# ScalarE's PSUM ring as four single banks, with exponentials, projections and the first MLP product in smaller units

## The chip, the cores and the metric

One core of a Trainium2 chip. The metric is device time in microseconds for one execution of the whole program; the median of several runs counts, and one more execution is profiled.

## The reference, cut to what matters

A PixArt-like stack over 16 items of 256 tokens with 128 channels, in float32. Layer 0, then an expert layer, then layers 2 and 3. Attention has 16 heads of 8 channels. Cross-attention goes to a context of 1601 tokens, self-attention to the item's own 256:

```python
def _attend(q, k, v):
    attn = jnp.einsum('bhnd,bhsd->bhns', q, k) * SCALE
    attn = jax.nn.softmax(attn, axis=-1)
    o = jnp.einsum('bhns,bhsd->bhnd', attn, v)
```

Around it stand layer norms with modulation by the item's condition, a projection with gate and residual, and in layers 0 and 3 an MLP of 512 hidden channels with a tanh GELU. Layer 0 has self- and cross-attention, layer 2 cross-attention, layer 3 both.

## The kernel before, in words

The function attention_phase runs twice: "pa" for layer 0, and "pb" for layers 2 and 3; the expert layer stands between them. Each phase carries two streams: "c", the cross-attention items (16 in pa, 32 in pb, 1601 keys in 13 tiles of 128, the last with 65), and "z", the self-attention items (16 in each, 256 keys). Each item goes through tokens: ln, xt (transpose), q, ctx (transposes of the context), k, v, M (maxima), Rn and Rt (the maxima as rows), S and T (scores), V (product with the values), oev and o (output moved and divided), ot, proj, and with an MLP ln2, x2t, h, tanh, gm, fc2. The function body_plan places the tokens of several items in one repeated body by the fractions of the PLACES tables, stage_list unrolls it, and merge_maxima moves the M tokens by a small model of the engines (class Clocks, with the work tables PE_WORK, ACT_WORK and DVE_WORK). Every engine walks the resulting list PROG in its order and waits on semaphores; so on each engine a waiting instruction holds up all behind it.

PSUM has eight banks. The ring of ScalarE (ACT) is two units of two banks, aunit, with RING_A = 2: every token of ACT_RING takes one unit, whether it fills 1024 columns or 256. VectorE's ring is three single banks (dbank), and one bank (obank) gathers the outputs of V. TensorE waits until the unit two tokens back has been emptied (a_free), writes, and signals a_full; ScalarE empties it and signals a_free.

A score unit S is four bf16 matmuls of 256 columns, two key tiles by two halves of the rows ("par"), and par is the bank of the unit. Its exponential is one instruction of 1024 columns (line 778). T is the same for the last tile. V is four float32 matmuls, in the trace as eight records, of one key tile. M is two matmuls of 512 columns in two banks of VectorE's ring, for stream z four of 256. The products ctx, k and v go in groups of 8 and 5 tiles (s.groups), h is eight records into 1024 columns with four evictions; GpSimd (POOL) then makes the cubic in z, and ScalarE the tanh.

An item of stream c has 48 S and 4 T, an item of stream z 8 S; the phases have 960 and 1792 such units.

## Time and profile before

| | |
|---|---|
| median of 3 runs | 5283.68 us (5279.14 to 5287.49) |
| span of the profiled execution | 5282.2 us |
| phase pa, about | 0 to 1740 us of the span |
| expert layer, about | 1740 to 2360 us |
| phase pb, about | 2360 to 5282 us |

The profiled execution has no time of its own beside its span; the span is 1.5 us under the median of the runs. Busy time of an engine is the union of its instructions. PE is TensorE's matmul side and PEld its weight loads; ends of pipelined matmuls are modelled, so matmuls that drain count as busy. DVE is VectorE, ACT ScalarE, POOL GpSimd. A wait is put down to the instruction whose signal came last.

### The profile page before, as it was taken

The page shows a single profiled execution, that of the slowest core. Times are in us where ns is not written, and L with a number is a line of the kernel's source. Part 1 is how long each engine was busy: PE and PEld are TensorE (multiplying, and loading weights), DVE is VectorE, ACT ScalarE, POOL GpSimd, SP SyncE. Part 2 cuts the span into 40 slices and gives each one's busy share as a digit, 9 for nine tenths or more (in the row PEclk, how much of TensorE's full clock was granted, in tenths as well). Part 3 has the DMA queues.
Part 4 walks back from the last instruction along what each step waited for, and adds up shares of the span by engine and source line. Part 5 has one row for each costly group of instructions (what it writes and reads, how often), then busy time and mean ns, then how long its engine had stood idle before and what let it go on. Part 6 is the DMA issues. An engine that isn't in the chain of part 4 may idle for free.

```text
span 5282.2 us, 123295 instructions
## 1 busy us (share of the span) xinstructions
PE 4674.1 (88%) x47956; PEld 2177.8 (41%) x47956; DVE 4160.5 (79%) x8997; ACT 3597.9 (68%) x4899; POOL 1667.0 (32%) x2339
## 2 busy tenths in 40 slices
PE   3799999999999588866999999999999999999997
PEld 1244444444443377752333333333333443333333
DVE  4598888888888244445999999999888888888884
ACT  1377777777777344432777777777787777777776
POOL 3443443443341100014233333242323233223321
PEclk9699999999999799986999999999999999999998
DMA  2221211211210111111121212121121211111110
GB/s 51 61 65 49 67 54 49 68 52 50 65 38 29 46 34 34 29 30 58 45 61 53 69 52 69 54 63 55 55 70 52 64 44 58 50 54 57 43 48 8
DMA packets 362976, 271.12 MB, mean 51 GB/s; under 512 B 47911, under 2 KB 325002, under 8 KB 362396
## 3 DMA queue, kind: packets, MB, share of 16 engines
q1 hardware_dynamic: 362396, 263.23, 17.3%
q8 instruction: 383, 6.28, 0.5%
q14 instruction: 197, 1.61, 0.1%
HBM read 86.96 MB, written 12.78 MB: 19 GB/s over the span
## 4 chain that ended last, share of the span: by engine, by line
PE 38%; DVE 7%; ACT 5%; issue 4%; POOL 0%; SPq 0%; DMA 0%; ACTq 0%; POOLq 0%; DVEq 0%
PE pb_obank L1027 14%; PE pb_dbank L1040 9%; PE pb_aunit L1003 6%; DVE pb_c_maxs L699 5%; ACT pb_probs L778 4%; PE pb_aunit L1081 2%; PE pb_aunit L1074 1%; PE pb_aunit L1066 1%; PE pb_dbank L1088 1%; PE pb_aunit L1114 1%; PE pb_aunit L1108 1%; PE pb_aunit L1011 1%; PE pb_aunit L1098 1%; DVE pb_c_mbf L709 1%; PE pb_aunit L1048 0%
## 5 line engine op out<-in xcount | busy, mean ns | idle before, releaser
L699 DVE TENSOR_REDUCE pb_c_maxs<-pb_dbank 128x1 f32<-128x512 f32 (+1 forms) x3584 | 2045.5, 627 | 312.2 <-PE pb_dbank L1040 293.4
L778 ACT ACTIVATE pb_probs<-pb_aunit 128x1024 f32<-128x1024 f32 (+1 forms) x1792 | 1761.6, 1024 | 276.2 <-PE pb_aunit L1003 223.8
L699 DVE TENSOR_REDUCE pa_c_maxs<-pa_dbank 128x1 f32<-128x512 f32 (+1 forms) x1792 | 1028.3, 627 | 181.5 <-PE pa_dbank L1040 167.6
L778 ACT ACTIVATE pa_probs<-pa_aunit 128x1024 f32<-128x1024 f32 (+1 forms) x960 | 937.4, 1024 | 194.9 <-PE pa_aunit L1003 160.6
L1027 PE MATMUL pb_obank<-pb_probs,pb_c_vaug 128*9 128x256 f32 x13312 | 945.6, 381 | 2.8 <-ACT pb_probs L778 0.2
L1040 PE MATMUL pb_dbank<-pb_c_kst,pb_c_qst 62*128 62x512 bf16 (+1 forms) x4096 | 760.6, 341 | 104.6 <-DVE pb_c_maxs L699 87.5
L1003 PE MATMUL pb_aunit<-pb_c_qst,pb_c_kst 64*128 64x256 bf16 x6144 | 581.2, 272 | 64.2 <-ACT pb_probs L778 40.6
L1040 PEld LDWEIGHTS pb_dbank<-pb_c_kst,pb_c_qst 62*128 62x128 bf16 x4096 | 227.7, 93 | 649.0 <-DVE pb_c_maxs L699 466.3
L1027 PE MATMUL pa_obank<-pa_probs,pa_c_vaug 128*9 128x256 f32 x6656 | 467.0, 381 | 1.3 <-ACT pa_probs L778 0.8
L1040 PE MATMUL pa_dbank<-pa_c_kst,pa_c_qst 62*128 62x512 bf16 (+1 forms) x2048 | 405.1, 348 | 44.9 <-DVE pa_c_maxs L699 21.1
L1027 PEld LDWEIGHTS pb_obank<-pb_probs,pb_c_vaug 128*9 128x9 f32 x13312 | 243.1, 89 | 372.3 <-issue 207.0
L1003 PEld LDWEIGHTS pb_aunit<-pb_c_qst,pb_c_kst 64*128 64x128 bf16 x6144 | 239.1, 95 | 338.8 <-ACT pb_probs L778 135.3
L1003 PE MATMUL pa_aunit<-pa_c_qst,pa_c_kst 64*128 64x256 bf16 x3072 | 289.3, 273 | 28.2 <-ACT pa_probs L778 17.6
L1040 PEld LDWEIGHTS pa_dbank<-pa_c_kst,pa_c_qst 62*128 62x128 bf16 x2048 | 116.4, 94 | 333.1 <-DVE pa_c_maxs L699 209.1
L699 DVE TENSOR_REDUCE pa_z_maxs<-pa_dbank 128x2 f32<-128x512 f32 x256 | 164.0, 684 | 51.9 <-PE pa_dbank L1040 51.5
L1027 PEld LDWEIGHTS pa_obank<-pa_probs,pa_c_vaug 128*9 128x9 f32 x6656 | 124.9, 89 | 181.8 <-issue 99.8
L1003 PEld LDWEIGHTS pa_aunit<-pa_c_qst,pa_c_kst 64*128 64x128 bf16 x3072 | 119.6, 95 | 163.5 <-ACT pa_probs L778 68.1
L699 DVE TENSOR_REDUCE pb_z_maxs<-pb_dbank 128x2 f32<-128x512 f32 x256 | 164.8, 686 | 11.7 <-PE pb_dbank L1040 8.8
L932 POOL TENSOR_TENSOR pb_z_x1a<-pb_z_x1a,pb_l_self_bo_rows 128x256 f32<-128x256 f32 x16 | 11.7, 731 | 490.8 <-ACT pb_z_x1a L848 490.8
L920 POOL CAST pb_c_ksp<-pb_c_kf 128x1024 bf16<-128x1024 f32 x64 | 54.5, 852 | 309.8 <-ACT pb_c_kf L821 309.8
L1532 DVE SCALAR_TENSOR_TENSOR moe_hh<-moe_ht,moe_hz 128x512 f32<-128x512 f32 x48 | 33.2, 692 | 123.6 <-ACT moe_ht L1626 122.8
L1658 POOL TENSOR_SCALAR moe_g<-moe_g2t 128x256 f32<-128x256 f32 x16 | 6.5, 406 | 369.5 <-ACT moe_g2t L1630 369.5
(475 smaller groups left out, 6737.6 us busy)
## 6 DMA issues: line engine op xcount, KB each, us to landing
pb_c_kst<-pb_c_ksp SPq DMA_DIRECT2D x384, 200.1 KB
pa_c_kst<-pa_c_ksp SPq DMA_DIRECT2D x192, 200.1 KB
pb_c_cin<-in_ctx SPq DMA_DIRECT2D x32, 768.0 KB
pa_c_cin<-in_ctx SPq DMA_DIRECT2D x16, 768.0 KB
moe_cin<-in_ctx SPq DMA_DIRECT2D x16, 768.0 KB
pb_c_qst<-pb_c_qsp SPq DMA_DIRECT2D x384, 32.0 KB
pa_z_qst<-pa_z_qsp SPq DMA_DIRECT2D x192, 32.0 KB
pa_z_kst<-pa_z_ksp SPq DMA_DIRECT2D x192, 32.0 KB
```

The lines of the kernel that those rows point to most:

```text
L699: dve.tensor_reduce(dst, dbank[N % RING_D][:, 0:cnt * width].rearrange("p (s c) -> p s c", s=cnt), AX.X, ALU.max).then_inc(d_free, 1)
L709: dve.tensor_copy(s.mbf[half][:], s.negm[half][:]).then_inc(s.m_bf, 1)
L778: act.activation(probs[u % RING_P][0:rows].rearrange("p a i q -> p (a i q)"), src[0:rows, :], ACT.Exp, scale=HD ** -0.5).then_inc(a_free, 1)
L920: pool.tensor_copy(s.ksp[:, 0, part], s.kf[:, part]).then_inc(s.k_hi, 1)
L1003: ins = pe.matmul(dst[:, par * 512 + h * NQ:par * 512 + (h + 1) * NQ], s.kst[b2][lo:lo + ROWS, pair, t * P:(t + 1) * P], s.qst[b2][lo:lo + ...
L1011: ins = pe.matmul(dst[0:s.last, par * 512 + pp * NQ:par * 512 + (pp + 1) * NQ], s.kst[b2][lo:lo + ROWS, 2 * q + pp, (s.kt - 1) * P:s.keys] ...
L1027: ins = pe.matmul(obank[32 * h4:32 * h4 + HD + 1, half * NQ:(half + 1) * NQ], s.vaug[i % 2][:, t, 4 * q + h4, :], src, start=(t == 0), sto ...
L1040: ins = pe.matmul(dbank[nd[tok, s.key, i, par] % RING_D][:, col:col + width], s.qst[b2][lo:lo + MAX_ROW, p, qt * P:(qt + 1) * P], s.kst[b2 ...
L1066: ins = pe.transpose(dst[:, (t - t0) * P:(t - t0) * P + rows], s.cin[0:rows, t, :], ident[0:rows, 0:rows])
L1074: ins = pe.matmul(dst[:, at - t0 * P:at - t0 * P + width], w.wkp[:], src[:, at:at + width], start=True, stop=True)
L1081: ins = pe.matmul(dst[0:rows, (t - t0) * P:(t - t0 + 1) * P], (s.srct if s.has_ctx else s.xmt)[:, t * P:t * P + rows], w.wv[:], start=True ...
L1088: ins = pe.transpose(dbank[N % RING_D][:, g * P:(g + 1) * P], s.osb[:, g, qt * P:(qt + 1) * P], ident[:])
```

## The change

ACT's ring becomes four single banks, abank, with RING_A = 4. S and T (TWO_BANKS) take two consecutive banks of the ring; every other token takes one. TensorE waits for the first bank ahead of the unit's first matmul and for the second ahead of its second, and signals each bank after its last matmul. ScalarE makes the exponential of each bank by itself, 512 columns, and frees each bank by itself. The groups of ctx, k and v become 4, 4, 4 and 1 tiles (GROUP = 4), and h two tokens of 512 columns, with GpSimd's part halved along with it; tanh stays one instruction. The added tokens stand 0.02 of a body behind their neighbours in PLACES. The work tables follow, Clocks knows single banks, and merge_maxima may now pull V tokens whose exponentials are done ahead of an S or T that would wait more than STALL.

```diff
@@ -169,8 +169,9 @@
         link.join()
 
 
-RING_A = 2
+RING_A = 4
 RING_D = 3
+GROUP = 4
 RING_P = 6
 K_ROWS = 48
...
-        self.groups = [(0, min(8, self.kt))] + ([(8, self.kt - 8)] if self.kt > 8 else [])
+        self.groups = [(t, min(GROUP, self.kt - t)) for t in range(0, self.kt, GROUP)]
...
-          "ca": 0.1616, "xt": 0.1932, "ln2": 0.1973, "v1": 0.2369, "st1": 0.2929, "q": 0.3211, "x2t": 0.3542, "h": 0.3645,
-          "tanh": 0.4567, "ctx0": 0.5124, "ldx": 0.6187, "gm": 0.6707, "ctx1": 0.7038, "ldc": 0.7509, "fc2": 0.8115,
-          "k0": 0.8271, "ldr": 0.8315, "k1": 0.889, "lda": 0.922, "st2": 0.9222, "Rt": (0.037, 0.0389)},
+    "c": {"kq": 0.0, "ln": 0.0131, "cs": 0.0316, "v0": 0.0441, "o0": 0.0515, "o1": 0.0537, "v1": 0.0641, "ot": 0.0689,
+          "proj": 0.1281, "ca": 0.1616, "xt": 0.1932, "ln2": 0.1973, "v2": 0.2369, "v3": 0.2569, "st1": 0.2929, "q": 0.3211,
+          "x2t": 0.3542, "h0": 0.3645, "h1": 0.3845, "tanh": 0.4567, "ctx0": 0.5124, "ctx1": 0.5324, "ldx": 0.6187,
+          "gm": 0.6707, "ctx2": 0.7038, "ctx3": 0.7238, "ldc": 0.7509, "fc2": 0.8115, "k0": 0.8271, "ldr": 0.8315,
+          "k1": 0.8471, "k2": 0.889, "k3": 0.909, "lda": 0.922, "st2": 0.9222, "Rt": (0.037, 0.0389)},
     "z": {"ln": 0.1012, "kq": 0.1471, "o0": 0.2, "o1": 0.2, "v0": 0.2511, "xt": 0.2788, "ldx": 0.4332, "lda": 0.6034,
           "ot": 0.7529, "proj": 0.7613, "q": 0.9575, "st1": 0.9607, "ldr": 0.98, "k0": 0.98, "Rt": (0.98, 0.1639)},
     "lead": 0.6052,
...
         at("q", 2, "q")
-        at("k0", 2, "k", 0)
-        at("v0", 1, "v", 0)
+        for name, off in (("k", 2), ("v", 1)) + ((("ctx", 2),) if s.has_ctx else ()):
+            for g in range(len(s.groups)):
+                at(f"{name}{g}", off, name, g)
...
             at("ca", 2, "ca")
-            at("ctx0", 2, "ctx", 0)
-            at("ctx1", 2, "ctx", 1)
-            at("k1", 2, "k", 1)
-            at("v1", 1, "v", 1)
             at("ln2", -1, "ln2")
             at("x2t", -1, "x2t")
-            at("h", -1, "h")
+            for part in range(MC // 2):
+                at(f"h{part}", -1, "h", part)
             at("tanh", -1, "tanh")
             at("gm", -1, "gm")
...
@@ -348,17 +348,19 @@
     return out
 
 
+TWO_BANKS = ("S", "T")
 ACT_RING = ("S", "T", "xt", "q", "ctx", "k", "v", "Rt", "ot", "proj", "x2t", "h", "fc2")
 
 
-PE_WORK = {"S": 0.23, "T": 0.23, "V": 0.52, "M": 0.23, "xt": 0.37, "q": 0.6, "ctx": (1.02, 0.63), "k": (1.9, 1.22), "v": (1.98, 1.31), "Rt": 0.25,
-           "o": 0.6, "ot": 0.37, "proj": 0.64, "x2t": 0.43, "h": 1.92, "fc2": 1.98}
-ACT_WORK = {"S": 1.03, "T": 1.03, "oev": 0.39, "xt": 0.39, "q": 0.94, "ctx": (1.02, 0.65), "k": (1.05, 0.7), "v": (1.03, 0.86), "Rt": 0.37,
-            "ot": 0.48, "proj": 0.38, "x2t": 0.59, "h": 1.9, "fc2": 0.38, "tanh": 1.05}
+PE_WORK = {"S": 0.23, "T": 0.23, "V": 0.52, "M": 0.23, "xt": 0.37, "q": 0.6, "ctx": 0.55, "k": 0.95, "v": 1.0, "Rt": 0.25,
+           "o": 0.6, "ot": 0.37, "proj": 0.64, "x2t": 0.43, "h": 1.0, "fc2": 1.98}
+ACT_WORK = {"S": 1.0, "T": 1.0, "oev": 0.39, "xt": 0.39, "q": 0.94, "ctx": 0.5, "k": 0.6, "v": 0.5, "Rt": 0.37,
+            "ot": 0.48, "proj": 0.38, "x2t": 0.59, "h": 0.95, "fc2": 0.38, "tanh": 1.05}
 DVE_WORK = {"M": 1.26, "Rn": 1.15, "ln": 1.0, "ln2": 1.0, "cs": 0.9, "ca": 2.2, "gm": 1.21, "o": 0.65}
 SELF_WORK = 0.5
 LATENCY, SLACK = 0.2, 0.25
 MAX_LATE, MAX_EARLY = 2, 12
+STALL = 0.1
...
@@ -366,21 +368,29 @@
     def __init__(self):
         self.pe = self.act = self.dve = 0.0
         self.a_free, self.d_free = [0.0] * RING_A, [0.0] * RING_D
+        self.done = {}
 
     def work(self, table, s, tok):
         w = table.get(tok[0], 0.0)
-        if tok[0] in ("ctx", "k", "v"):
-            return (w[tok[1]] if s.has_ctx else SELF_WORK) if w else 0.0
+        if tok[0] in ("ctx", "k", "v") and w:
+            return w * s.groups[tok[1]][1] / GROUP
         return w
 
     def banks_free(self):
         return max(self.d_free[-RING_D], self.d_free[1 - RING_D])
 
-    def take(self, tok, s):
+    def scores_wait(self):
+        return self.a_free[1 - RING_A] - self.pe
+
+    def values_ready(self, tok, s, i):
+        tail = s.last < P and tok[2] == s.kt - 1
+        return self.done.get((("T", tok[1]) if tail else ("S", tok[1], tok[2] // 2, 1), s.key, i), 1e9) <= self.pe
+
+    def take(self, tok, s, i):
         k = tok[0]
         tail = k == "M" and s.units[tok[2]][0][2] < P
         if k in ACT_RING:
-            self.pe = max(self.pe, self.a_free[-RING_A])
+            self.pe = max(self.pe, self.a_free[1 - RING_A if k in TWO_BANKS else -RING_A])
         if k == "M":
             self.pe = max(self.pe, self.banks_free())
         if k == "o":
@@ -388,8 +398,12 @@
         self.pe += self.work(PE_WORK, s, tok) * (0.4 if tail else 1.0)
         act, dve = self.work(ACT_WORK, s, tok), self.work(DVE_WORK, s, tok) * (0.45 if tail else 1.0)
         if act:
-            self.act = (max(self.act, self.pe + LATENCY) if k != "tanh" else self.act) + act
-            if k in ACT_RING:
+            start = max(self.act, self.pe + LATENCY) if k != "tanh" else self.act
+            self.act = start + act
+            self.done[tok, s.key, i] = self.act
+            if k in TWO_BANKS:
+                self.a_free += [start + act / 2, self.act]
+            elif k in ACT_RING:
                 self.a_free.append(self.act)
         if dve:
             start = max(self.dve, self.pe + LATENCY) if k in ("M", "o") else self.dve
@@ -405,7 +419,7 @@
     clocks, out, late, used = Clocks(), [], [], set()
 
     def put(item):
-        clocks.take(item[0], item[1])
+        clocks.take(*item)
         out.append(item)
 
     for n, item in enumerate(prog):
@@ -425,6 +439,16 @@
                         used.add(m)
                         put(prog[m])
                     break
+        if tok[0] in TWO_BANKS:
+            reach = n + 1
+            while reach < min(len(prog), n + 8) and clocks.scores_wait() > STALL and clocks.banks_free() > clocks.pe:
+                if reach not in used:
+                    if prog[reach][0][0] == "V" and clocks.values_ready(*prog[reach]):
+                        used.add(reach)
+                        put(prog[reach])
+                    elif prog[reach][0][0] not in ("S", "T", "M"):
+                        break
+                reach += 1
         put(item)
     return out
 
...
@@ -433,9 +457,11 @@
 
     PROG = merge_maxima(stage_list(streams, late_x, places))
     na, nd, ns, nv, no, out_before, values_before = {}, {}, {}, {}, {}, {}, {}
+    banks = 0
     for tok, s, i in PROG:
         if tok[0] in ACT_RING:
-            na[tok, s.key, i] = len(na)
+            na[tok, s.key, i] = banks
+            banks += 2 if tok[0] in TWO_BANKS else 1
         if tok[0] == "M":
             nd[tok, s.key, i, 0] = len(nd)
             nd[tok, s.key, i, 1] = len(nd)
...
-        return na[tok, s.key, i] + 1
+        return na[tok, s.key, i] + (2 if tok[0] in TWO_BANKS else 1)
...
 
-        aunit = [ctx.enter_context(nc.psum_tensor(f"{nm}_aunit{i}", [P, 1024], F32)) for i in range(RING_A)]
+        abank = [ctx.enter_context(nc.psum_tensor(f"{nm}_abank{i}", [P, 512], F32)) for i in range(RING_A)]
...
@@ -768,15 +794,16 @@
                 w = spec.w
                 if k in ACT_RING:
                     N = na[tok, s.key, i]
-                    src = aunit[N % RING_A]
+                    src = abank[N % RING_A]
                 if k in ("S", "T"):
                     u = ns[tok, s.key, i]
                     rows = s.last if k == "T" else P
-                    act.wait_ge(a_full, N + 1)
                     if u >= RING_P:
                         act.wait_ge(pv, last_value(s_order[u - RING_P]) + 1)
-                    act.activation(probs[u % RING_P][0:rows].rearrange("p a i q -> p (a i q)"), src[0:rows, :], ACT.Exp,
-                                   scale=HD ** -0.5).then_inc(a_free, 1)
+                    for par in range(2):
+                        act.wait_ge(a_full, N + par + 1)
+                        act.activation(probs[u % RING_P][0:rows, par].rearrange("p i q -> p (i q)"), abank[(N + par) % RING_A][0:rows, :], ACT.Exp,
+                                       scale=HD ** -0.5).then_inc(a_free, 1)
                 elif k == "oev":
                     q = tok[1]
                     half = streams.index(s)
...
-                    ins = act.activation(s.vaug[i % 2][:, t0:t0 + full, :, 0:HD], part[:, 0:full], ACT.Identity)
+                    part = src[:].rearrange("p (t h d) -> p t h d", t=GROUP, d=HD)
+                    if full:
+                        ins = act.activation(s.vaug[i % 2][:, t0:t0 + full, :, 0:HD], part[:, 0:full], ACT.Identity)
                     if full < cnt:
                         ins = act.activation(s.vaug[i % 2][0:s.last, s.kt - 1, :, 0:HD], part[0:s.last, full], ACT.Identity)
...
                                    scale=column(s.dcols, spec.mlp["cols"][0])).then_inc(a_free, 1)
                 elif k == "h":
                     act.wait_ge(a_full, N + 1)
-                    wait(act, s.g_h, s.mlp_to[i])
-                    for c in range(MC):
-                        ins = act.activation(s.z[:, c, :], src[:, c * NQ:(c + 1) * NQ], ACT.Identity, bias=w.b1_half[:, c:c + 1], scale=0.5)
+                    if tok[1] == 0:
+                        wait(act, s.g_h, s.mlp_to[i])
+                    for c in range(2):
+                        at = 2 * tok[1] + c
+                        ins = act.activation(s.z[:, at, :], src[:, c * NQ:(c + 1) * NQ], ACT.Identity, bias=w.b1_half[:, at:at + 1], scale=0.5)
                     ins.then_inc(a_free, 1)
                 elif k == "tanh":
-                    act.wait_ge(s.g_p, 3 * (s.mlp_to[i] + 1))
+                    act.wait_ge(s.g_p, 3 * (MC // 2) * (s.mlp_to[i] + 1))
                     act.activation(s.hg[:], s.hg[:], ACT.Tanh, scale=2.0 * GELU_SCALE).then_inc(s.g_e, 1)
                 elif k == "fc2":
                     act.wait_ge(a_full, N + 1)
...
-                    j = s.mlp_to[i]
+                    part = slice(2 * tok[1], 2 * tok[1] + 2)
+                    j = 2 * s.mlp_to[i] + tok[1]
                     pool.wait_ge(a_free, a_done(tok, s, i))
-                    if j:
+                    if j > 1 and tok[1] == 0:
                         pool.wait_ge(a_full, a_done(("fc2",), s, i - 1))
-                    pool.tensor_tensor(s.hg[:], s.z[:], s.z[:], ALU.mult).then_inc(s.g_p, 1)
+                    pool.tensor_tensor(s.hg[:, part], s.z[:, part], s.z[:, part], ALU.mult).then_inc(s.g_p, 1)
                     pool.wait_ge(s.g_p, 3 * j + 1)
-                    pool.tensor_scalar(s.hg[:], s.hg[:], 4 * GELU_CUBE, 1.0, ALU.mult, ALU.add).then_inc(s.g_p, 1)
+                    pool.tensor_scalar(s.hg[:, part], s.hg[:, part], 4 * GELU_CUBE, 1.0, ALU.mult, ALU.add).then_inc(s.g_p, 1)
                     pool.wait_ge(s.g_p, 3 * j + 2)
-                    pool.tensor_tensor(s.hg[:], s.hg[:], s.z[:], ALU.mult).then_inc(s.g_p, 1)
+                    pool.tensor_tensor(s.hg[:, part], s.hg[:, part], s.z[:, part], ALU.mult).then_inc(s.g_p, 1)
                 elif k == "fc2":
                     j = s.mlp_to[i]
                     pool.wait_ge(a_free, a_done(tok, s, i))
...
                     N = na[tok, s.key, i]
-                    dst = aunit[N % RING_A]
+                    dst = abank[N % RING_A]
                     wait(pe, a_free, N - RING_A + 1)
+                    pair_dst = (dst, abank[(N + 1) % RING_A])
                 if k == "S":
                     _, q, j, pp = tok
                     pair = 2 * q + pp
@@ -1000,17 +1032,23 @@
                         for par in range(2):
                             t = 2 * j + h
                             lo = par * ROWS
-                            ins = pe.matmul(dst[:, par * 512 + h * NQ:par * 512 + (h + 1) * NQ], s.kst[b2][lo:lo + ROWS, pair, t * P:(t + 1) * P],
+                            if h == 0 and par == 1:
+                                wait(pe, a_free, N - RING_A + 2)
+                            ins = pe.matmul(pair_dst[par][:, h * NQ:(h + 1) * NQ], s.kst[b2][lo:lo + ROWS, pair, t * P:(t + 1) * P],
                                             s.qst[b2][lo:lo + ROWS, pair, :], start=True, stop=True)
-                    ins.then_inc(a_full, 1)
+                            if h == 1:
+                                ins.then_inc(a_full, 1)
                 elif k == "T":
                     q = tok[1]
                     for pp in range(2):
                         for par in range(2):
                             lo = par * ROWS
-                            ins = pe.matmul(dst[0:s.last, par * 512 + pp * NQ:par * 512 + (pp + 1) * NQ], s.kst[b2][lo:lo + ROWS, 2 * q + pp, (s.kt - 1) * P:s.keys],
+                            if pp == 0 and par == 1:
+                                wait(pe, a_free, N - RING_A + 2)
+                            ins = pe.matmul(pair_dst[par][0:s.last, pp * NQ:(pp + 1) * NQ], s.kst[b2][lo:lo + ROWS, 2 * q + pp, (s.kt - 1) * P:s.keys],
                                             s.qst[b2][lo:lo + ROWS, 2 * q + pp, :], start=True, stop=True)
-                    ins.then_inc(a_full, 1)
+                            if pp == 1:
+                                ins.then_inc(a_full, 1)
                 elif k == "V":
                     _, q, t = tok
                     tail = s.last < P and t == s.kt - 1
...
                     pe.wait_ge(a_free, a_done(("x2t",), s, i))
-                    for c in range(MC):
-                        ins = pe.matmul(dst[:, c * NQ:(c + 1) * NQ], w.w1[:, c * P:(c + 1) * P], s.x2t[:], start=True, stop=True)
+                    for c in range(2):
+                        at = 2 * tok[1] + c
+                        ins = pe.matmul(dst[:, c * NQ:(c + 1) * NQ], w.w1[:, at * P:(at + 1) * P], s.x2t[:], start=True, stop=True)
                     ins.then_inc(a_full, 1)
                 elif k == "fc2":
```

Also in the diff, not shown: the PLACES entries of layer 0, changed in the same way, and one notation of a source slice.

## Rows read from the trace of the kernel before

**Rows 1.** The page: busy time by engine, and the two groups of exponentials.
```profile
PE 4674.1 (88%) x47956; PEld 2177.8 (41%) x47956; DVE 4160.5 (79%) x8997; ACT 3597.9 (68%) x4899; POOL 1667.0 (32%) x2339
...
L778 ACT ACTIVATE pb_probs<-pb_aunit 128x1024 f32<-128x1024 f32 (+1 forms) x1792 | 1761.6, 1024 | 276.2 <-PE pb_aunit L1003 223.8
...
L778 ACT ACTIVATE pa_probs<-pa_aunit 128x1024 f32<-128x1024 f32 (+1 forms) x960 | 937.4, 1024 | 194.9 <-PE pa_aunit L1003 160.6
```

**Rows 2.** Windows: length, busy PE, PEld, DVE, ACT, POOL, clock, DMA.
```profile
100.00:1640.00 1540.00, 1409.87 (x14847) 611.75 (x14846) 1305.75 (x2908) 1108.79 (x1453) 631.08 (x907) 0.96 0.20 56
...
2480.00:5250.00 2770.00, 2574.93 (x28978) 1077.20 (x28977) 2427.22 (x4957) 2132.83 (x2658) 851.25 (x1166) 1.00 0.19 54
```

**Rows 3.** Who waited for the exponentials of line 778: us, times.
```profile
  PEld pb_aunit L1003: 148.2, 332
  PEld pa_aunit L1003: 74.4, 188
  PEld pb_obank L1027: 53.3, 219
  PE pb_aunit L1003: 43.0, 125
...
  PE pa_aunit L1003: 19.7, 69
  PEld pa_aunit L1048: 18.3, 37
  PEld pb_aunit L1081: 15.3, 34
  PEld pb_aunit L1048: 12.3, 20
  PEld pb_aunit L1066: 11.3, 18
```

**Rows 4.** Waits within 2480 to 5250 us: us, times, longest.
```profile
PE pb_dbank L1040 <- DVE pb_c_maxs L699: 94.2, 180, 1.3
...
ACT pb_c_vaug L831 <- PE pb_aunit L1081: 56.9, 62, 2.7
...
ACT pb_c_kf L821 <- PE pb_aunit L1074: 37.2, 60, 2.0
...
DVE pb_c_maxs L699 <- PE pb_dbank L1040: 262.5, 488, 3.4
```

**Rows 5.** The chain of waits within 2480 to 5250 us, by line.
```profile
by line: PE pb_obank L1027 26.6%; PE pb_dbank L1040 15.9%; PE pb_aunit L1003 12.2%; DVE pb_c_maxs L699 9.5%; ACT pb_probs L778 8.4%; issue 7.3%; PE pb_aunit L1081 4.1%; PE pb_aunit L1074 2.2%; PE pb_dbank L1088 2.0%; PE pb_aunit L1066 1.9%;
```

**Rows 6.** Timeline of ACT: start, length, instruction, count.
```profile
3555.67 3.85 ACT L778 ACTIVATE pb_probs<-pb_aunit 128x1024 f32<-128x1024 f32 x4
...
3564.68 1.02 ACT L778 ACTIVATE pb_probs<-pb_aunit 128x1024 f32<-128x1024 f32 x1 [0.73 <-PE pb_aunit L1003]
3566.27 0.60 ACT L831 ACTIVATE pb_c_vaug<-pb_aunit 128x512 f32<-128x512 f32 x1 [0.57 <-PE pb_aunit L1081]
3566.77 0.26 ACT L833 ACTIVATE pb_c_vaug<-pb_aunit 65x128 f32<-65x128 f32 x1
```

**Rows 7.** Timeline of PE: maxima and scores of stream z, V, v.
```profile
3563.37 0.39 PE L1040 MATMUL pb_dbank<-pb_z_kst,pb_z_qst 62*128 62x256 bf16 x4
3563.69 0.62 PE L1027 MATMUL pb_obank<-pb_probs,pb_c_vaug 128*9 128x256 f32 x8
3564.24 0.39 PE L1003 MATMUL pb_aunit<-pb_z_qst,pb_z_kst 64*128 64x256 bf16 x4
...
3564.86 1.38 PE L1081 MATMUL pb_aunit<-pb_l_cross_wv,pb_c_srct 128*128 128x128 f32 x10
```

**Rows 8.** Timeline around a product for v of eight tiles.
```profile
4003.49 1.26 DVE L699 TENSOR_REDUCE pb_c_maxs<-pb_dbank 128x1 f32<-128x512 f32 x2
...
4003.55 2.05 PE L1081 MATMUL pb_aunit<-pb_l_cross_wv,pb_c_srct 128*128 128x128 f32 x16
...
4005.63 1.03 ACT L831 ACTIVATE pb_c_vaug<-pb_aunit 128x1024 f32<-128x1024 f32 x1 [0.70 <-PE pb_aunit L1081]
...
4005.95 1.29 DVE L699 TENSOR_REDUCE pb_c_maxs<-pb_dbank 128x1 f32<-128x512 f32 x2 [1.21 <-PE pb_dbank L1040]
```

**Rows 9.** Timeline of an item's MLP: GpSimd's last product and the tanh.
```profile
4320.06 2.35 POOL L962 TENSOR_TENSOR pb_c_hg<-pb_c_hg,pb_c_z 128x1024 f32<-128x1024 f32 x1
4323.29 1.04 ACT L862 ACTIVATE pb_c_hg<-pb_c_hg 128x1024 f32<-128x1024 f32 x1
```

More of the change, by code:

```diff
@@ L670, in _ @@
                         dve.tensor_copy(dst[:, par * ROWS:(par + 1) * ROWS].rearrange("p (d b) -> p d b", b=PAIRS),
-                                        src.rearrange("p (b par d) -> p par d b", par=2, d=HD)[:, par])
+                                        src[:].rearrange("p (b par d) -> p par d b", par=2, d=HD)[:, par])
                 if spec.mlp:
@@ L829, in _ @@
                     full = cnt if t0 + cnt < s.kt or s.last == P else cnt - 1
-                    part = src[:].rearrange("p (t h d) -> p t h d", t=8, d=HD)
-                    ins = act.activation(s.vaug[i % 2][:, t0:t0 + full, :, 0:HD], part[:, 0:full], ACT.Identity)
+                    part = src[:].rearrange("p (t h d) -> p t h d", t=GROUP, d=HD)
+                    if full:
+                        ins = act.activation(s.vaug[i % 2][:, t0:t0 + full, :, 0:HD], part[:, 0:full], ACT.Identity)
                     if full < cnt:
```

11 rows, old and new, of tables (PLACES_LAYER0, PLACES_LAYERS23) are left out of this document.

## The prediction

> **What bounds the kernel now.** I read the page's shares first, then the windows, the view of waits, the chain, and last short timelines. In [rows 1] TensorE is busy 88% of the span, VectorE 79%, ScalarE 68%. No one engine explains the end, so the two attention phases have to be looked at alone: they hold all that the diff touches. [Rows 2] has both, without their filling and their emptying. In the second, 2770 us long, TensorE is busy 2575 (93%), VectorE 2427 (88%) and ScalarE 2133 (77%). The reader should see three engines that are all close to full, and one queue (TensorE's, in an order fixed beforehand) that feeds the other two. A gap of 0.5 us anywhere costs something if it falls on the queue, and nothing otherwise.
>
> Who holds TensorE up? [Rows 3] shows it for the exponentials: weight loads of scores waited for an exponential 148.2 us in 332 places in the second phase and 74.4 us in 188 in the first, 222.6 us in all, and four small units 57.2 us in 109. Of the 222.6 only 62.7 us (43.0 and 19.7) are idle time of the matmuls themselves; the rest passes while earlier matmuls drain. VectorE's side is heavier: 94.2 us of TensorE idle in the second phase alone [rows 4]. The other way round, VectorE waits 262.5 us for maxima. The chain of waits says the same in shares of that phase [rows 5]: about 65% on TensorE's lines, 9.5% on VectorE's maxima, 8.4% on exponentials, 7.3% in hand-over. So a change of ScalarE's ring reaches a part of the time, and what it frees runs into VectorE next.
>
> **The exponentials: a cost.** Each of the 1792 and 960 units of 1024 columns [rows 1] becomes two of 512. An exponential of 1024 columns takes 1.02 us; four in a row take 3.85 [rows 6], so in a stream (3.85 - 1.02) / 3 = 0.94. No exponential of 512 columns is there. The nearest row is an eviction of 128x512 in 0.60 us whose follower starts 0.50 after it [rows 6]. Two halves in a stream then take 1.00 to 1.04, alone 0.60 + 0.50 = 1.10: I take +0.08 per unit. Over 2752 units that is 220 us of ScalarE work, all of it on the path only if ScalarE were. By the chain 8.4% of 2770 = 233 us of exponentials are on it, 226 units, and 226 x 0.08 = 18 us. The first phase, in proportion to its units (960/1792), adds 10. **+30 us**, bounds 0 and 220. The rest is covered by ScalarE's idle time (2770 - 2133 = 637 us); its busy share rises to about 84%. If that cover is gone the price is the 220.
>
> The Trainium skill ("ScalarE: Activation LUTs", What ACT_TABLE_LOAD costs) prices an ACTIVATE with immediate scale at 186 ns plus 0.833 ns a column, with 93 ns overlapped by the next. By it a split costs 93 ns and the total work would be 256 us instead of 220; the term on the path would be 33 us. It speaks against the change by a little more than the row does.
>
> **Scores on TensorE.** The same four matmuls, with a second wait ahead of the second and two signals. The trace has the twin of this form: the maxima of the short stream, four matmuls of 256 columns on alternating row halves, with a wait in the same place and two signals, take 0.39 us, the scores 0.39 [rows 7]. So 0, with the 0.01 that the view resolves as upper bound: 28 us over 2752 units. The second bank comes free no earlier than the whole unit did, so between scores that follow each other nothing is won: the order still blocks at the second matmul.
>
> **More groups: a cost on TensorE.** ctx, k and v go from 2 to 4 groups for each item of the long stream (+6), and h from 1 to 2 where there is an MLP (+1): 32 x 6 + 16 in the second phase and 16 x 7 in the first, 320 more units. v with 16 matmul records takes 2.05 us [rows 8] and with 10 1.38 [rows 7]: 0.112 each, with 0.26 fixed, of which I put 0.07 under the next group's start. 320 x 0.19 = 61 us; two thirds of it lie on the chain as TensorE does: **+40 us**, bounds 0 and 83 (320 x 0.26). ScalarE has 320 x 0.08 = 26 us more, inside its idle time. GpSimd's products come in the same sum of columns; it is busy 851 of 2770 us [rows 2]. The DMAs of k wait for the last group only, as now. Behind ScalarE's wait at tanh the exponentials queue; today GpSimd ends at 4320.06 + 2.35 = 4322.41 and tanh starts at 4323.29 [rows 9]. Halves let GpSimd start while the second half is made, so this margin of 0.9 us does not shrink. 0.
>
> **The ring: the gain.** A small unit takes one bank instead of two. Behind two scores it can start when the first half of the older is out, 0.5 us earlier; scores right behind a small unit need half a unit less room, again 0.5. For the four kinds of small unit that is all of their 57.2 us. For scores I need the share of waits right behind a small unit; small units are about a quarter of all, and waits gather behind them, so 0.4 is my choice: 0.4 x 222.6 = 89. Together 146 us of weight-load waits. If only the share that is matmul idle counts (62.7 / 222.6 = 0.28) it is 41. With VectorE at 88% close behind, I take a value nearer the lower end: **-60 us**, bounds -41 and -146.
>
> **Shorter blocks: a gain.** The product for v holds TensorE 2.05 us; meanwhile VectorE runs out, having 1.26 us of maxima in hand, and idles 1.21, ScalarE 0.70 [rows 8]. In [rows 4] v and k make ScalarE wait 56.9 and 37.2 us, and the product h is as long. Blocks of this length that get halved: v, k for 48 items, h for 32, 128 in all. Halved they are about as long as what VectorE has in hand. 128 x 0.7 (2.0 less 1.3) = 90 us of VectorE idle; about half is felt, since TensorE has also to catch up: **-45 us**, bounds 0 and -90.
>
> **The planner.** It may now pull products with V ahead of scores that would wait over 0.1 us. Just behind two scores V waits for the same exponential as the scores do, so there is nothing ready to pull; behind a small unit there is. What is left of the scores' matmul idle, 0.6 x 62.7 = 38 us, is the most to win; pulled V (0.55 us) can make the scores late by as much. **-10 us**, bounds -38 and +20. The rest of the order shifts with the new work tables; I price that at 0, within the same bounds.
>
> **Sum:** +30 +40 -60 -45 -10 = -45 us on the profiled execution's span of 5282.2. The median of the runs shown is 5283.7, 1.5 us above, so the forecast is 5239, rounded to 5240.
>
> **Rivals.** (1) *ScalarE becomes the bound, slower.* All of 246 us (220 + 26) is felt against gains of 115: +131, 5415 us. For: 84% is close to VectorE's 88%, and V needs the second half 0.08 later. Against: it idles 637 us in the second phase, and only 8.4% of the chain is its exponentials. It decides, if the 40 us of extra groups are kept, from (115 - 40) / 0.08 = 940 units on the path, a third of 2752; by the chain there are 226 and about 120. Chance 0.20. (2) *VectorE takes what TensorE gains:* no change, 5284. For: its waits are the largest cause of idle TensorE in [rows 4]. Against: its own 262.5 us of waiting say that it is fed late. 0.10. (3) *The ring was the coupling:* the gains come at 146 + 90 + 38 = 274 against costs of 70, 5080 us. 0.06. (4) *TensorE pays for each added signal and unit:* scores 28, groups 83, gains at 41 + 0, exponentials 30: +100, 5384. Against: the two rows at 0.39. 0.08, half of it within reach of no more than +40.
> The Trainium skill ("TensorE: Matmul & The Clock Gate", The cost: per-tile semaphore tail) gives 26.3 ns for every increment. By it the added signals would cost 2752 x 0.026 = 72 us and turn the sum to +27; the rows at 0.39 for either form do not show it. It is the page's form of rival 4.
>
> **How the numbers follow.** The forecast's own case (gains as sized, -10 to -150) has 0.56; its range is 5130 to 5272. With rival 3 faster by over 0.2% has 0.62, which is about what a measurement of this kernel can tell from no change; within 0.2% 0.10; slower 0.28 by rivals 1 and 4. The range 5120 to 5375 leaves out most of rival 3 and about half of rival 1.
>
> **What would show it.** Right: exponentials of 512 columns at 0.59 to 0.60 us alone and near 0.5 in a stream; ScalarE's busy time up by some 240 us; waits of weight loads for exponentials down from 222.6 to some 130 and the small ones nearly gone; VectorE's 262.5 down by 50 or more; four-matmul scores still 0.39. Wrong: an exponential of 512 in a stream above 0.55, waits of V on exponentials well above today's 53.3 us [rows 3], or VectorE's maxima waiting more than now because the order of the plan got worse.

## The result, and the profile after

The changed kernel takes 5316.93 us (median of 4 runs) where the kernel before took 5284.76 beside it: a ratio of 1.0059, interval 1.0047 to 1.0071. It is 32 us slower. The forecast was 45 us faster. The profiled execution spans 5316.0 us.

The page of the changed kernel, its shares and the exponentials:

```profile
PE 4782.7 (90%) x47956; PEld 2203.0 (41%) x47956; DVE 4100.7 (77%) x8997; ACT 3769.1 (71%) x7891; POOL 1747.3 (33%) x2819
...
L805 ACT ACTIVATE pb_probs<-pb_abank 128x512 f32<-128x512 f32 (+1 forms) x3584 | 1877.7, 610 | 239.3 <-PE pb_abank L1037 209.3
...
L805 ACT ACTIVATE pa_probs<-pa_abank 128x512 f32<-128x512 f32 (+1 forms) x1920 | 999.1, 604 | 189.6 <-PE pa_abank L1037 158.0
```

Its windows, with the columns of [rows 2]:

```profile
100.00:1640.00 1540.00, 1423.21 (x14689) 611.17 (x14689) 1266.81 (x2880) 1146.09 (x2388) 654.06 (x1071) 0.96 0.20 56
...
2500.00:5270.00 2770.00, 2635.16 (x28803) 1090.33 (x28801) 2392.89 (x4953) 2234.07 (x4573) 896.34 (x1448) 1.00 0.19 54
```

Who waited for its exponentials (us, times), to be held against [rows 3]:

```profile
  PEld pb_abank L1037: 195.9, 553
  PEld pb_obank L1065: 106.5, 395
  PEld pa_abank L1037: 99.3, 285
  PEld pa_obank L1065: 63.8, 231
...
  PE pb_abank L1037: 20.6, 95
```

Waits of TensorE and VectorE within 2500 to 5270 us, against [rows 4]:

```profile
PE pb_dbank L1078 <- DVE pb_c_maxs L725: 68.6, 178, 1.1
...
DVE pb_c_maxs L725 <- PE pb_dbank L1078: 296.6, 553, 3.8
```

Timeline of its ScalarE, against [rows 6]:

```profile
3500.22 1.08 ACT L805 ACTIVATE pb_probs<-pb_abank 128x512 f32<-128x512 f32 x2 [0.56 <-PE pb_abank L1037]
...
3501.90 3.06 ACT L805 ACTIVATE pb_probs<-pb_abank 128x512 f32<-128x512 f32 x6
```

Idle time of TensorE has become busy time. TensorE is idle less for the exponentials (20.6 us of matmul idle in the second phase for 43.0), and yet it is busy 60 us longer in a window of the same length. Part of that is a unit of scores that stands half written while it waits for its second bank; that is counted as busy (the scores of stream c are busy 654.7 us in the second phase for 581.2). So the fall of the matmul idle time is not a gain by itself. And the waits that the ring should have shortened have grown: weight loads of scores wait 295.2 us for 222.6, those of V 106.5 for 53.3 in the second phase. VectorE waits 296.6 us for its maxima, for 262.5. ScalarE, with more to do, waits slightly less for scores than before (209.3 and 158.0 us for 223.8 and 160.6 [rows 1]). The queue of TensorE looks fuller, and it feeds VectorE worse.

### The profile page after: what moved, and what is told of

It is laid out like the page before. It is cut to its first block, busy times and chain, and to the rows that moved or that the text cites. A ratio compares the mean times of both kernels' runs of the same rounds, so it can differ in the third digit from the quotient of the medians.

```text
span 5316.0 us, 127115 instructions
## 1 busy us (share of the span) xinstructions
PE 4782.7 (90%) x47956; PEld 2203.0 (41%) x47956; DVE 4100.7 (77%) x8997; ACT 3769.1 (71%) x7891; POOL 1747.3 (33%) x2819
## 4 chain that ended last, share of the span: by engine, by line
PE 40%; DVE 7%; ACT 5%; issue 2%; POOL 1%; SPq 0%; DMA 0%; ACTq 0%; POOLq 0%; DVEq 0%
PE pb_obank L1065 14%; PE pb_dbank L1078 9%; PE pb_abank L1037 7%; DVE pb_c_maxs L725 5%; ACT pb_probs L805 5%; PE pb_abank L1112 2%; PE pb_abank L1119 2%; PE pb_dbank L1126 1%; PE pb_abank L1104 1%; PE pb_abank L1153 1%; PE pb_abank L1136 1%; PE pb_abank L1048 1%; PE pb_abank L1086 1%; PE pb_abank L1147 0%; PE pb_abank L1095 0%
## 5 line engine op out<-in xcount | busy, mean ns | idle before, releaser
L725 DVE TENSOR_REDUCE pb_c_maxs<-pb_dbank 128x1 f32<-128x512 f32 (+1 forms) x3584 | 2049.1, 627 | 350.1 <-PE pb_dbank L1078 327.0
L805 ACT ACTIVATE pb_probs<-pb_abank 128x512 f32<-128x512 f32 (+1 forms) x3584 | 1877.7, 610 | 239.3 <-PE pb_abank L1037 209.3
L725 DVE TENSOR_REDUCE pa_c_maxs<-pa_dbank 128x1 f32<-128x512 f32 (+1 forms) x1792 | 1027.2, 627 | 225.0 <-PE pa_dbank L1078 214.2
L805 ACT ACTIVATE pa_probs<-pa_abank 128x512 f32<-128x512 f32 (+1 forms) x1920 | 999.1, 604 | 189.6 <-PE pa_abank L1037 158.0
L1078 PE MATMUL pb_dbank<-pb_c_kst,pb_c_qst 62*128 62x512 bf16 (+1 forms) x4096 | 788.4, 341 | 83.9 <-DVE pb_c_maxs L725 67.1
L1037 PE MATMUL pb_abank<-pb_c_qst,pb_c_kst 64*128 64x256 bf16 x6144 | 654.7, 273 | 35.6 <-ACT pb_probs L805 20.6
L1078 PEld LDWEIGHTS pb_dbank<-pb_c_kst,pb_c_qst 62*128 62x128 bf16 x4096 | 243.0, 93 | 627.7 <-DVE pb_c_maxs L725 463.1
L1037 PEld LDWEIGHTS pb_abank<-pb_c_qst,pb_c_kst 64*128 64x128 bf16 x6144 | 274.1, 95 | 356.8 <-ACT pb_probs L805 183.1
L1037 PE MATMUL pa_abank<-pa_c_qst,pa_c_kst 64*128 64x256 bf16 x3072 | 327.0, 274 | 22.7 <-ACT pa_probs L805 14.1
L1037 PEld LDWEIGHTS pa_abank<-pa_c_qst,pa_c_kst 64*128 64x128 bf16 x3072 | 135.2, 95 | 194.6 <-ACT pa_probs L805 94.1
L950 POOL CAST pb_c_ksp<-pb_c_kf 128x512 bf16<-128x512 f32 (+1 forms) x128 | 66.2, 517 | 276.8 <-ACT pb_c_kf L848 276.7
L859 ACT ACTIVATE pb_c_vaug<-pb_abank 128x512 f32<-128x512 f32 x96 | 59.0, 615 | 100.8 <-PE pb_abank L1119 100.8
```

What stands on the lines that cost most here:

```text
L725: dve.tensor_reduce(dst, dbank[N % RING_D][:, 0:cnt * width].rearrange("p (s c) -> p s c", s=cnt), AX.X, ALU.max).then_inc(d_free, 1)
L805: act.activation(probs[u % RING_P][0:rows, par].rearrange("p i q -> p (i q)"), abank[(N + par) % RING_A][0:rows, :], ACT.Exp, scale=HD ** ...
L859: ins = act.activation(s.vaug[i % 2][:, t0:t0 + full, :, 0:HD], part[:, 0:full], ACT.Identity)
L950: pool.tensor_copy(s.ksp[:, 0, part], s.kf[:, part]).then_inc(s.k_hi, 1)
L1037: ins = pe.matmul(pair_dst[par][:, h * NQ:(h + 1) * NQ], s.kst[b2][lo:lo + ROWS, pair, t * P:(t + 1) * P], s.qst[b2][lo:lo + ROWS, pair, : ...
L1078: ins = pe.matmul(dbank[nd[tok, s.key, i, par] % RING_D][:, col:col + width], s.qst[b2][lo:lo + MAX_ROW, p, qt * P:(qt + 1) * P], s.kst[b2 ...
```

## The experiments

Each was timed in five rounds beside the kernel before, whose median lay at 5279.8 to 5281.5 us in these series. "+47" below is the difference of the two medians of one series. A "list" is PROG, the order in which all engines walk the tokens; it depends only on the planner, so a kernel can be given another one's list.

**The split alone**, on the kernel before:

```diff
-                    act.activation(probs[...] , src[0:rows, :], ACT.Exp, scale=HD ** -0.5).then_inc(a_free, 1)
+                    for par in range(2):
+                        ins = act.activation(probs[...][0:rows, par] , src[0:rows, par * 512:(par + 1) * 512], ACT.Exp, scale=HD ** -0.5)
+                    ins.then_inc(a_free, 1)
```

> The kernel before, with every exponential of 1024 columns made as two of 512 and one signal after the second; ring, groups and order untouched. Theory P (the split itself holds the queues up: the unit is complete 0.06 to 0.08 us later, and V and the next scores wait for that): 25 to 45 us slower than before, some 5310 to 5330. Theory Q (the split is hidden in ScalarE's idle time, and the loss comes from the order of TensorE's queue): within 10 us of before. By the prediction's own term it is +30.

5326.75 us, ratio 1.0089 (1.0075 to 1.0103): **+47**, just above what Theory P allowed; Theory Q has fallen. The list is the same, so this is the price of the second instruction. Weight loads of scores now wait 292.8 us, matmuls of scores 92.4 us idle:

```profile
  PEld pb_aunit L1005: 192.4, 425
  PEld pa_aunit L1005: 100.4, 239
  PE pb_aunit L1005: 63.1, 179
...
  PE pa_aunit L1005: 29.3, 90
```

**The groups alone**, on the kernel before: GROUP = 4, h in halves, and the planner's entries for them, every token still in a whole unit of two banks.

> The kernel before, with only the groups of four tiles and h in halves, each still in a whole unit of the ring of two. By the prediction's terms -45 for shorter blocks and +40 for more units, so within 10 us of before. Theory P says the same. Theory R (extra units cost more than shorter blocks give, because each breaks a run of bf16 products on TensorE): 15 to 40 us slower, with VectorE's maxima waiting longer than 431 us in all.

5286.82, ratio 1.0012 (1.0003 to 1.0021): **+7**, within the 10 us of the prediction's terms; Theory R's 15 to 40 did not come. Only the sum of shorter blocks and extra units is measured here, and the planner makes another list for them. The waits that shorter blocks should have cut have grown; within 2480 to 5250 us, against 262.5 and 56.9 in [rows 4]:

```profile
DVE pb_c_maxs L699 <- PE pb_dbank L1044: 299.9, 595, 4.4
...
ACT pb_c_vaug L832 <- PE pb_aunit L1085: 111.8, 62, 3.2
```

**Split and groups together** on the old ring:

> The kernel before with both the split exponentials and the groups of four, on the old ring of two units. Alone they cost 47 and 7 us. If they add, 5334 (+54), and the ring of single banks, which is all that then separates this kernel from the changed one without pulls (5284), gives 50 us. If the split only hurts where long groups start, or the two share one wait, 5290 to 5315, and the ring gives less than 30.

5338.78, ratio 1.0112 (1.0099 to 1.0126): **+59**. They add, with 5 us on top.

**The changed kernel without pulls:**

```diff
-STALL = 0.1
+STALL = 1e9
```

> The changed kernel with the planner's new rule switched off (STALL so large that no V is pulled ahead of scores). The rule moves 327 V tokens and makes 143 more separate blocks of V. Theory Q (those blocks cost 0.2 us each on TensorE and make scores late): 20 to 40 us faster than the changed kernel, so near 5285. Theory P (the exponentials are the cause): within 10 us of the changed kernel, or slower, since the pulls fill waits.

5283.93, ratio 1.0005 (0.9996 to 1.0014): **+4**. The pulls cost 28 us.

**Two other ways to pull.** In pairs (a V token goes only if its twin can go with it), and only where the modelled wait is over 0.5 us (STALL = 0.5):

> The changed kernel with the planner pulling V only in pairs, both V tokens of one macro together. It pulls more V tokens (496 instead of 327), yet TensorE's queue has fewer separate blocks of V: 1773, against 2011 in the changed kernel and 1868 without pulls. Theory F (what costs is each further block of V, 0.22 us): 95 blocks fewer than without pulls, so 10 to 25 us faster than 5284, near 5265. Theory L (pulled V makes the scores behind it late and starves ScalarE): more V is pulled, in chunks of 0.98 us, so slower than the changed kernel's 5317.

> The changed kernel with STALL at 0.5 us instead of 0.1, so that V (0.55 us) is pulled only where the modelled wait is about as long as V itself: 88 pulls, 1942 blocks of V, 74 more than without pulls. Theory F: 74 x 0.22 = 16 us slower than without pulls, near 5300. Theory L: no score becomes late, so within 5 us of 5284 or faster.

Pairs: 5426.08, ratio 1.0274 (1.0260 to 1.0288), **+146**. Late pulls: 5285.32, 1.0012 (1.0003 to 1.0021), **+5**. Theory F, blocks of V, has fallen: the list with the fewest blocks is by far the slowest. Theory L's forecasts held for both. In the kernel with pairs ScalarE idles 442.3 us before exponentials, waiting for scores, where without pulls it is 323.3; in the changed kernel it is 367.3 (209.3 and 158.0). First with pairs, then without pulls:

```profile
  PE pb_abank L1044: 272.1, 437
  PE pa_abank L1044: 170.2, 262
```

```profile
  PE pb_abank L1037: 187.0, 369
  PE pa_abank L1037: 136.3, 181
```

But VectorE starves as much. Its waits for the maxima of stream c are 497.0 us without pulls (301.5 and 195.5), 541.2 in the changed kernel (327.0 and 214.2) and 633.1 with pairs (390.0 and 243.1). So it is shown that pulled V holds up what stands behind it in TensorE's queue; that ScalarE is the one that counts, as Theory L says, is not. The second phase without pulls and with pairs:

```profile
L725 DVE TENSOR_REDUCE pb_c_maxs<-pb_dbank 128x1 f32<-128x512 f32 (+1 forms) x3584 | 2047.2, 626 | 326.9 <-PE pb_dbank L1078 301.5
L732 DVE TENSOR_REDUCE pb_c_maxs<-pb_dbank 128x1 f32<-128x512 f32 (+1 forms) x3584 | 2053.3, 626 | 419.4 <-PE pb_dbank L1085 390.0
```

In the timeline of the kernel with pairs ScalarE stands still for two units' length:

```profile
3508.07 2.10 ACT L812 ACTIVATE pb_probs<-pb_abank 128x512 f32<-128x512 f32 x4
3512.22 1.09 ACT L812 ACTIVATE pb_probs<-pb_abank 128x512 f32<-128x512 f32 x2 [2.05 <-PE pb_abank L1044]
```

**The opposite rule**, one unit of scores ahead of V where ScalarE is about to run out, on the kernel without pulls:

```diff
+        if tok[0] == "V" and clocks.act < clocks.pe + 1.5 and clocks.a_free[1 - RING_A] <= clocks.pe:
+            ...   # the next S or T goes first
```

> The changed kernel without pulls, and with the opposite rule: where the model sees ScalarE run out within 1.5 us and both banks free, one unit of scores goes ahead of V (252 units). Theory L (late scores starve ScalarE, 0.1 to 0.3 us for each pulled V) expects a gain if that also holds from this side: 10 to 40 us faster than 5284. If ScalarE's queue was long enough there, no change within 5 us; if it is VectorE or the later V that then waits, 10 to 40 us slower.

5301.02, ratio 1.0041 (1.0027 to 1.0054): **+21**, 17 slower than without it. So scores earlier than the plan has them are no gain either.

**Same list on both rings.** The single banks under the list of the split-and-groups kernel, and the old ring under the list of the kernel without pulls:

```diff
+PLAN_A = 2      # the planner's own ring: class Clocks and merge_maxima of the kernel before
 RING_A = 4
-ACT_WORK = {"S": 1.0, "T": 1.0,
+ACT_WORK = {"S": 1.03, "T": 1.03,
```

> The ring of single banks with its halves, but with every engine walking the list that the planner made for the old ring (the list of the split-and-groups kernel, token for token). Theory M (the ring itself gives the 55 us between 5339 and 5284): 5275 to 5300. Theory O (the order planned with the changed model gives it): 5320 to 5340.

> The other corner: the old ring of two units with split exponentials and groups of four, walking the list planned for single banks (without pulls). Theory M: 5330 to 5360, as this ring can only be slower under a list that is not its own. Theory O: 5285 to 5300.

Single banks, old list: 5232.86, ratio 0.9912 (0.9899 to 0.9926), **-47**. Old ring, new list: 5388.02, ratio 1.0205 (1.0191 to 1.0219), **+108**. Theory O has fallen: the new list costs time on either ring. Theory M was right that the ring gives the gain, but both times lie outside its ranges, since the ring gives twice the 55 us and the list takes the other half back. With the list held, the ring gives 106 us (+59 to -47) or 104 (+108 to +4); with the ring held, the new list costs 49 or 51. The first of these is the fastest kernel of the study, 0.88% ahead of the kernel before. What the ring does is seen in its waits for exponentials, first on the old ring with the same list, then on single banks:

```profile
  PEld pb_aunit L1009: 247.9, 483
  PEld pa_aunit L1009: 120.2, 233
  PE pb_aunit L1009: 94.4, 212
  PE pa_aunit L1009: 47.9, 105
```

```profile
  PEld pb_abank L1018: 186.8, 508
  PEld pa_abank L1018: 88.1, 266
  PEld pb_obank L1046: 82.3, 317
...
  PE pb_abank L1018: 23.6, 100
```

Matmul idle before scores falls from 94.4 to 23.6 in the second phase, and weight-load waits from 368.1 to 274.9 in both; those of V grow from 42.0 to 82.3 in the second. Part of the fall only moves into the matmuls' busy time, by the half written units: the scores of stream c are busy 669.6 us for 588.5. A cleaner sign is VectorE, which waits 60 us less for maxima in the second phase:

```profile
L699 DVE TENSOR_REDUCE pb_c_maxs<-pb_dbank 128x1 f32<-128x512 f32 (+1 forms) x3584 | 2052.7, 626 | 375.7 <-PE pb_dbank L1046 357.6
L706 DVE TENSOR_REDUCE pb_c_maxs<-pb_dbank 128x1 f32<-128x512 f32 (+1 forms) x3584 | 2043.5, 626 | 319.1 <-PE pb_dbank L1059 297.7
```

**What in the ring gives it.** One exponential of 1024 columns wherever the two banks lie side by side (1948 of the 2752 units), two of 512 where the unit wraps: on the changed kernel, without pulls, and on the kernel at 5233.

> The changed kernel with one exponential of 1024 columns wherever the two banks of the unit lie side by side in the ring (three positions of four), and two of 512 only where the unit wraps around. Theory P: most of the split's cost comes back, 20 to 35 us faster than the changed kernel. Theory Q: within 10 us of it, since the order stays and half a unit's earlier release is lost as well.

> Single banks, no pulls, and one exponential of 1024 columns where the two banks lie side by side. With pulls that made the changed kernel 28 us slower. If the halves' own early release and early start are what the ring lives on, this is as much slower than 5284: 5305 to 5320. If it was an effect of the pulls alone (they counted on the earlier end), within 8 us of 5284 or faster.

> The 5233 kernel, same list token for token, with one exponential of 1024 columns where the two banks lie side by side. If the release by halves carries the ring's gain: 5270 to 5290, since 50 us were lost by this step under the new list too. If the small units' single banks carry it: 5200 to 5225, as most of the split's 47 us come back.

5345.19 (ratio 1.0124, 1.0110 to 1.0137), **+65**; 5334.02 (1.0106, 1.0091 to 1.0121), **+54**; 5291.46 (1.0017, 1.0008 to 1.0026), **+10**. Against the same lists with halves that is 33, 50 and 57 us worse, although ScalarE is spared most of the second instructions. All three are slower than any theory allowed, the last by 1.5 us only. It has the list of the groups kernel, which with whole units of two banks is at +7. Its 804 units that still are made in halves cost some 14 us by the split's price (an estimate, 47 x 804 / 2752), so single banks for small units are worth some 10 us at most as long as most units of scores come free as a whole; the halves carry the gain.

**Both banks first**: TensorE waits for both banks ahead of a unit's first matmul, on the kernel without pulls.

> The changed kernel without pulls, with TensorE waiting for both banks ahead of a unit's first matmul, so that no unit stands half written. If the first matmul ahead of the second wait gives something, this is 5 to 25 us slower than 5284; if the ring's gain comes only from small units and from the early start of ScalarE, within 5 us of it.

5293.51, ratio 1.0023 (1.0014 to 1.0032): **+13**, 9 slower. The half written unit is worth 9 us of the ring's gain. Beside the old ring under the same list (5388.02) this kernel is 94.5 us faster, and no unit stands half written in either, so here the fall of the waits is real. Second phase, old ring first:

```profile
  PEld pb_aunit L1036: 269.3, 503
...
  PE pb_aunit L1036: 110.4, 252
```

```profile
  PEld pb_abank L1035: 229.0, 492
...
  PE pb_abank L1035: 65.7, 160
```

**What in the new list costs.** The planner's slack, which sets how early maxima may go, from 0.25 to 0.40 us on three kernels: the changed kernel without pulls, the kernel at 5233, and the kernel before:

> The changed kernel without pulls, with the planner's SLACK at 0.40 us instead of 0.25, which lets maxima go while their banks are still modelled as busy for 0.4 us. Counted against the order before merging, the maxima then stand on average 0.94 (first phase) and 0.47 (second) scores earlier, where the list of 5284 has 0.13 earlier and 0.49 later and the list of 5233 0.39 earlier and 0.30 later. Theory D (a list is slow as its maxima stand late, so that VectorE runs out): 5225 to 5260. Theory E (it is something else in the new model): 5275 to 5300, and if TensorE then waits for VectorE more than VectorE gains, above 5300.

> The 5233 kernel (single banks under the old planner's list), with SLACK at 0.40: maxima 1.07 and 0.60 scores earlier. Theory D: faster again, 5200 to 5225. Theory E: 5225 to 5260. The best version if D holds.

> The kernel before with SLACK at 0.40 and nothing else: maxima 0.94 and 0.37 scores earlier, where they stand 0.17 earlier and 0.57 later. Theory D: 15 to 40 us faster than before. Theory E: within 10 us of it.

5314.19 (1.0063, 1.0050 to 1.0076), **+33**; 5279.09 (0.9995, 0.9986 to 1.0004), **-2**; 5274.84 (0.9988, 0.9979 to 0.9997), **-7**. Theory D has fallen: on single banks earlier maxima cost 29 and 45 us. Then the two differences between the planners, the table and the rules. The first kernel has the new rules and a table with longer entries than either planner had, the second the old rules and the new planner's entry for scores:

> The changed kernel without pulls, with the planner's rules for single banks kept and its ScalarE table set to lengths that the traces show (unit of scores 1.10, ctx 0.70, k 0.69, v 0.61). Theory N (the table is too short, so the model sees ScalarE free when it is not): 5230 to 5255. Theory R (the rule of banks that come free by halves makes the list): 5275 to 5295.

> The 5233 kernel, whose list comes from the old rules of two whole units, with the scores' entry in the planner's table at 1.00 instead of 1.03 as in the changed kernel. Theory N: 5255 to 5285. Theory R: 5225 to 5245.

Longer entries for ScalarE in the new planner: 5273.73 (0.9988, 0.9979 to 0.9997), **-7**, 11 better than +4. The shorter entry in the old planner: 5247.73 (0.9936, 0.9923 to 0.9948), **-33**, 14 worse than -47. Both lie between the ranges of Theory N and Theory R. So the table's entry makes 14 of the 51 us, and the rules of the ring in the model the other 37, by subtraction.

## Why the prediction was wrong

The runs give this ladder from the kernel before: split and groups +59, single banks with halves -106, the new planner's list +51, pulls +28, in sum +32. The time lies inside the stated range of 5120 to 5375, but on the side that had a chance of 0.28, by rivals that did not happen; that is luck.

- **The exponentials.** Predicted +30, bounds 0 and 220; measured +47. The durations were right: 0.60 us alone, (3.06 - 0.60) / 5 = 0.49 in a stream, 1.08 for a unit alone. ScalarE's busy time rose by 171 us, where 246 were expected. The share on the path was larger than the chain of the kernel before said, since that chain also grows: in the split-only kernel exponentials are 11.8% of it, for 8.4% [rows 5]. By the prediction's own rule that would be some 37 us (an estimate: 11.8% of 2770 us in units of 1.08 us, times 0.08, and 960/1792 of that for the first phase). The chain of the split-only kernel within 2500 to 5270 us:

```profile
by line: PE pb_obank L1029 24.9%; PE pb_dbank L1042 15.1%; ACT pb_probs L779 11.8%; PE pb_aunit L1005 11.7%; DVE pb_c_maxs L699 8.4%; issue 8.2%; PE pb_aunit L1083 4.0%; PE pb_aunit L1076 2.3%; PE pb_dbank L1090 2.0%; PE pb_aunit L1068 1.7%
```

- **Scores on TensorE.** Predicted 0, and borne out: waiting ahead of the first matmul instead of the second is 9 us worse, so the added wait does no harm. The second signal was not timed by itself, but under one list the scores of stream c are busy 869.1 us with one signal on the old ring and 879.1 with two and both waits first, 0.004 us more for each of 2304 units; the timeline of the changed kernel still has four in 0.39 us. Nothing bears out the 72 us that the prediction works out from the Trainium skill ("TensorE: Matmul & The Clock Gate", The cost: per-tile semaphore tail).
- **More groups and shorter blocks.** Predicted +40 and -45, sum -5; measured +7 together. The two were not told apart. VectorE's idle time did not fall in any kernel with groups, and ScalarE's wait for v rose from 56.9 to 111.8 us, so the shorter blocks gave less than thought. Since the sum came out near the forecast, the extra units must have cost less too, which no run shows; that the sum is right is luck.
- **The ring.** Predicted -60, bounds -41 and -146; measured -106 and -104, within the bounds. The part of the mechanism that concerns scores, half a unit's earlier release, fits the runs: the gain needs both the single banks and the halves. A part may be ScalarE's earlier start on the first half; this was not separated from the release. The part that concerns small units is not borne out: "all of their 57.2 us" should have gone, but under one list the weight loads of ctx, k and v wait 23.2, 19.8 and 17.1 us for exponentials on the old ring and 24.4, 25.1 and 14.7 on single banks, in the second phase. As to the size, I chose a value near the lower end, from the waits of the kernel before. The other edits raise them before the ring lowers them: matmul idle before scores is 62.7 us, 92.4 with the split, 110.9 with the groups and 142.3 with both.
- **The planner.** This is the step that failed: "-10 us, bounds -38 and +20" for the pulls, and "I price that at 0, within the same bounds" for the rest of the order. They cost 28 and 51. On the pulls I had named the danger, that pulled V makes the scores late, and then sized it like the gain. The rest of the order I had not looked into at all, though every line of the planner's model is in the diff. The prediction's last sign of being wrong, VectorE's maxima waiting more because the order got worse, is what came, and so did the one before it: weight loads of V wait 106.5 us for 53.3.

Of the rivals none describes what happened. Rival 1 had all of 246 us of added ScalarE work felt; with split and groups together it was 59. Without the planner's part the kernel is 47 us faster, 2 us from the forecast's -45, but that is luck, a sum of terms that missed on both sides.

Open is what in the new rules costs 37 us. It is not the number of separate blocks of V, and not a mean lateness of the maxima: counted as in the expectations, the list with the longer entries has them 0.31 scores earlier and 0.24 later, about where the list of 5233 has them (0.39 and 0.30), and is 41 us slower. The lists differ in where maxima stand among scores, and each was made to fit a model of waits; why the old model's fits the new ring better was not found.

## What to carry to other kernels

A static order that a model plans is part of the kernel: when the model is changed along with a buffer, time the new buffer under the old order before anything else. Work moved ahead to fill a modelled wait also delays everything behind it in the same queue; here 327 moves of 0.55 us cost 28 us and 496 cost 142. And size a gain on the waits of the kernel that has the other edits in it, not on those of the kernel before. Where a group of matmuls can wait in its middle, hold two traces against each other by the waits of the engines that it feeds, since its own idle time is hidden.

## What was not expected of the hardware

One more instruction for each unit costs ScalarE 0.04 us in a stream (0.98 for 0.94 [rows 6]) and 0.06 alone. Over 2752 units it added 150 us of busy time in the split-only kernel (3747.5 for 3597.9) and 47 us to the end: a third of it is felt, on an engine that is idle 30% of the span. TensorE's busy share misleads as well: it rose from 88% to 90% with a kernel that got slower, since scores that wait for their second bank count as busy. Without pulls it is 4749.9 us, and under the same list with both waits ahead of the unit 4667.8, 82 us less busy in a kernel that takes 9 us longer:

```profile
PE 4749.9 (90%) x47956; PEld 2209.6 (42%) x47956; DVE 4102.1 (78%) x8997; ACT 3769.3 (71%) x7891; POOL 1751.2 (33%) x2819
PE 4667.8 (88%) x47956; PEld 2154.1 (41%) x47956; DVE 4101.1 (77%) x8997; ACT 3771.6 (71%) x7891; POOL 1750.0 (33%) x2819
```
